# Attention blocks of one batch per core, eight key groups instead of nine, and three slots copied by register address

## What is computed

```python
xn = layernorm(x)                                    # x: 2 batches x 4096 tokens x 2048
q  = xn @ w_dq.T @ w_uq.T                            # 16 heads of 128
k, v = split(xn @ w_dkv.T @ w_ukv.T)                 # through a 512-wide latent
attn = softmax(causal(q k^T / sqrt(128))) @ v @ w_out.T
wq(w) = clip(round(w / mean|w|), -1, 1) * mean|w|    # w_gate, w_up: 8192 x 2048, w_down: 2048 x 8192
aq(x) = clip(round(x * s), -128, 127) / s, s = 127 / max|x| of the row
h  = silu(aq(xn) @ wq(w_gate).T) * (aq(xn) @ wq(w_up).T)
x  = x + attn + aq(h) @ wq(w_down).T
```

## Time and profile before

| | us |
|---|---|
| median of 3 runs | 2411.6 |
| all runs | 2411.1, 2411.6, 2578.09 |
| profiled execution, as a run | 2432.53 |
| its span on the slowest core (core 2) | 2431.0 |
| spans of the 8 cores | 2392.5 to 2431.0 |
| PE busy | 2336.6 (96%) |
| DVE busy | 1243.7 (51%) |
| ACT busy | 1166.3 (48%) |
| POOL busy | 120.9 (5%) |
| mean DMA rate | 237 GB/s |

### The profile page before, as it was taken

One profiled execution on the slowest core, in us unless ns is written; L12 is line 12 of the kernel. 1 busy time (PEld: TensorE's weight loads), 2 busy tenths in 40 slices (PEclk: granted clock), 3 DMA queues, 4 the chain that ended last, 5 costly groups with the idle time before them and its releaser, 6 DMA issues.

```text
span 2431.0 us, 41168 instructions; the slowest of 8 cores (2392.5 to 2431.0 us)
## 1 busy us (share of the span) xinstructions
PE 2336.6 (96%) x14556; PEld 1215.1 (50%) x14556; DVE 1243.7 (51%) x1668; ACT 1166.3 (48%) x1343; POOL 120.9 (5%) x227
## 2 busy tenths in 40 slices
PE   4999899999999998999999999999998999999998
PEld 2554444677777775444444444444443444444443
DVE  6883522788888874444444444444435454322222
ACT  3763311577777775445444454444542255332220
POOL 0000110000000000000000000000000100000000
PEclk9999888999999999999999999999999999999999
DMA  9875785688888837976777767777644977875551
GB/s 279 279 205 112 187 188 159 225 283 276 274 281 274 278 106 215 306 276 246 280 271 264 273 245 279 272 265 271 246 187 147 266 258 296 273 261 195 203 196 70
DMA packets 88707, 575.27 MB, mean 237 GB/s; under 512 B 10114, under 2 KB 10114, under 8 KB 25538
## 3 DMA queue, kind: packets, MB, share of 16 engines
q1 hardware_dynamic: 57490, 391.47, 46.6%
q0 software_dynamic: 31024, 181.16, 23.7%
HBM read 551.62 MB, written 48.23 MB: 247 GB/s over the span
## 4 chain that ended last, share of the span: by engine, by line
PE 80%; DMA 9%; DVE 6%; issue 3%; ACT 2%; SPq 0%; DVEq 0%; ACTq 0%; POOL 0%; POOLq 0%
PE pp L1100 36%; PE pp L1158 13%; PE pp L948 7%; PE pp L979 4%; PE pp L983 4%; PE pp L920 4%; PE pp L1043 3%; PE pp L1017 3%; DMA aos<-aob 2%; DMA hpair<-hs 2%; DMA xr<-xk 2%; DVE accTw L609 2%; PE pp L1113 1%; PE pp L1167 1%; DMA ust<-wut 1%
## 5 line engine op out<-in xcount | busy, mean ns | idle before, releaser
L1100 PE MATMUL pp<-xqfm,tw 128*128 128x512 bf16 x4096 | 886.0, 380 | 0.0
L1100 PEld LDWEIGHTS pp<-xqfm,tw 128*128 128x128 bf16 x4096 | 401.1, 98 | 484.0 <-issue 2.1
L474 ACT ACTIVATE ptile<-pp 128x512 bf16<-128x512 f32 (+3 forms) x576 | 313.3, 561 | 158.3 <-PE pp L1014 79.5
L742 DVE TENSOR_TENSOR hst<-pp,gs 128x1024 f32<-128x1024 f32 x64 | 78.4, 1224 | 351.9 <-PE pp L1100 346.6
L1043 PE MATMUL pp<-vg,ptile 128*128 128x129 bf16 x2112 | 213.8, 220 | 0.3 <-ACT ptile L474 0.2
L486 ACT ACTIVATE twi<-gst,thr 128x2048 int16<-128x2048 f32 x62 | 124.1, 2002 | 165.3 <-PE pp L1100 149.9
L494 ACT ACTIVATE gs<-gs 128x1024 f32<-128x1024 f32 x64 | 67.6, 1056 | 278.5 <-DVE gs L735 278.5
L609 DVE TENSOR_REDUCE accTw<-svr 128x1 f32<-128x1024 f32 x166 | 200.8, 1210 | 0.0
L507 ACT ACTIVATE td2i<-dst,thr 128x2048 int16<-128x2048 f32 x48 | 96.1, 2002 | 210.2 <-PE pp L1158 164.9
L1043 PEld LDWEIGHTS pp<-vg,ptile 128*128 128x128 bf16 x2112 | 151.8, 98 | 62.1 <-issue 5.5
L979 PE MATMUL pp<-ckv,wukv 128*128 128x512 bf16 x576 | 169.5, 383 | 6.4 <-DVE kg L616 5.4
(11 more groups left out here) (171 smaller groups left out, 2616.7 us busy)
## 6 DMA issues: line engine op xcount, KB each, us to landing
gst<-wgt SPq DMA_DIRECT2D x64, 1024.0 KB, 7.9
ust<-wut SPq DMA_DIRECT2D x64, 1024.0 KB, 10.7
dst<-wdt SPq DMA_DIRECT2D x64, 1024.0 KB, 5.8
sgb<-wdt POOLq DMA_DIRECT2D x62, 1024.0 KB, 11.0
svr<-wgt SPq DMA_DIRECT2D x52, 1024.0 KB, 7.5
xr<-xk SPq DMA_DIRECT2D x36, 1024.0 KB, 8.6
ssr<-wut POOLq DMA_DIRECT2D x33, 1024.0 KB, 7.8
svr<-wut SPq DMA_DIRECT2D x31, 1024.0 KB, 7.0
```

Source lines behind the costliest of these rows:

```text
L474: e.activation(out=ptile[:, n % 4, q0:512], in_=banks[3 + n % 3][:, q0:512], func=AF.Exp, scale=SCALE, bias=EXPB).then_inc(ex_s, 1)
L1100: mm = e.matmul(out=banks[b0 + half], lhsT=tw[:, n % 3, gu, fc, :], rhs=xqfm[:, 4 * half:4 * half + 4, fc, :], start=(fc == 0), stop=(fc = ...
```

## The change

Core c now takes blocks c % 4 and 7 - c % 4 of one batch, c // 4. Both need keys of the same batch, so the core projects that batch's eight groups once (NK = 4096, NKC = 32), its own two first and then the others in order. The two causal triangles and the past still make NT = 36 attention tiles a head: 8 diagonal ones ("d"), 16 of the later query block against the lower own block and the first three other groups ("f"), and 12 in three slots ("m"), in which both the key group and the query block differ by core. [...] A K or V evacuation of a later head waits for POOL's copies of the head whose buffer it overwrites. The sums of the weight blocks are divided anew: NU 8 to 12, NV 83 to 74, NS 35 to 42 (six half sums a head instead of five), NG 62 to 60, and G's sums stand two steps earlier in the gate and up loop. POOL's ssr loads are issued three a head, in one program with the copies.

```diff
-NK = 4608
-NKC = 36
+NK = 4096
+NKC = 32
+NT = 36
-TILES = [0, 4, 1, 5, 2, 6, 3, 7] + list(range(8, NKC))
+TILES = [("d", 4 * (i % 2) + i // 2) for i in range(8)] + [("f", i) for i in list(range(4)) + list(range(8, 20))] + \
+    [("m", i) for i in range(12)]
...
-    fl = [f for j in range(9) for f in (("k", h + 1, j), ("v", h + 1, j))] if h + 1 < HN else []
+    fl = [f for j in range(8) for f in (("k", h + 1, j), ("v", h + 1, j))] if h + 1 < HN else []
...
-NF, NU, NV, NS = 4, 8, 83, 35
+NF, NU, NV, NS = 4, 12, 74, 42
-V_AFTER = (1, 2, 4, 5, 7, 8, 10, 11, 13, 14, 16, 17)
-S_AFTER = (3, 9, 15, 22, 29)
+V_AFTER = (1, 2, 4, 5, 7, 8, 10, 11, 13, 14)
+S_AFTER = (3, 8, 14, 19, 25, 30)
...
         for k in range(NU):
-            e.wait_ge(qp_mm, 2 * (QCD + 2 * k))
+            e.wait_ge(qp_mm, 2 * (QCD + 3 * k // 2))
...
+        def move_slots(h):
+            e.wait_ge(kv_ev, ITEM_NO["v", h, 7])
+            if h >= 1:
+                e.wait_ge(sc_mm, NT * h)
+                e.wait_ge(pv_mm, NT * h)
+            for s in range(3):
+                e.tensor_copy(out=kdyn[:, s, :], in_=kg[:, h % 2, bass.ds(moved[s], 512)])
+                m = e.tensor_copy(out=vdyn[:, s, :, :].rearrange("p j c -> p (j c)"),
+                                  in_=vg[:, h % 2, :, :].rearrange("p j c -> p (j c)")[:, bass.ds(moved[3 + s], 520)])
+            m.then_inc(dy_p, 1)
+
         e.wait_ge(qp_mm, 2 * (QCD + FD))
-        for b in range(NS):
-            if b >= S_RING:
-                e.wait_ge(p_s, 2 * (b - S_RING + 1))
-            e.dma_start(out=ssr[:, b % S_RING, :], in_=scale_blocks[S_FIRST + b]).then_inc(s_in[b % S_RING], 16)
-        e.wait_ge(pv_mm, NKC * HN)
+        for h in range(HN):
+            if h >= 1:
+                move_slots(h)
+            for b in range(3 * h, min(3 * h + 3, NS)):
+                if b == 2:
+                    move_slots(0)
+                if b >= S_RING:
+                    e.wait_ge(p_s, 2 * (b - S_RING + 1))
+                e.dma_start(out=ssr[:, b % S_RING, :], in_=scale_blocks[S_FIRST + b]).then_inc(s_in[b % S_RING], 16)
+        e.wait_ge(pv_mm, NT * HN)
...
-            if 4 <= n < NG + 2:
-                e.wait_ge(p_g, n - 3)
-                e.dma_start(out=sgb[:, n % 2, :], in_=scale_blocks[G_FIRST + n - 2]).then_inc(pg_in[n % 2], 16)
+            if 2 <= n < NG:
+                e.wait_ge(p_g, n - 1)
+                e.dma_start(out=sgb[:, n % 2, :], in_=scale_blocks[G_FIRST + n]).then_inc(pg_in[n % 2], 16)
...
-            if 6 <= st < NG + 6:
-                n = st - 6
+            if 4 <= st < NG + 4:
+                n = st - 4
...
+            if kind != "o" and i >= 2:
+                e.wait_ge(dy_p, i - 1)
...
-            e.tensor_copy(out=qcur[:, h % 2, :], in_=qfm[:, h, :]).then_inc(qw_v, 1)
-            e.wait_ge(qw_v, h + 1)
+            e.tensor_copy(out=qcur[:, h % 2, :], in_=qfm[:, h, :]).then_inc(qc_v, 1)
+
+        def q_move(h):
+            e.wait_ge(qc_v, h + 1)
+            if h >= 1:
+                e.wait_ge(sc_mm, NT * h)
             for s in range(3):
-                c = e.tensor_copy(out=qdyn[:, h % 2, s, :], in_=qcur[:, h % 2, bass.ds(qsel[s], 512)])
-            c.then_inc(qc_v, 1)
+                m = e.tensor_copy(out=qdyn[:, s, :], in_=qcur[:, h % 2, bass.ds(qsel[s], 512)])
+            m.then_inc(dq_q, 1)
...
+            if kind == "m":
+                e.wait_ge(dy_p, h + 1)
+                e.wait_ge(dq_q, h + 1)
+                kt = kdyn[:, key // 4, 128 * (key % 4):128 * (key % 4) + 128]
...
 def halves_of(c):
-    pair = ((0, c), (1, 7 - c))
-    return pair if c >= 4 else (pair[1], pair[0])
+    return (c // 4, c % 4), (c // 4, 7 - c % 4)
```

More of the change, by code:

```diff
@@ L373, in pool_prog @@
                 e.dma_start(out=wukv[:, cc, :], in_=wukv_d[cc * 128:(cc + 1) * 128, :]).then_inc(wu_c, 16)
-        e.wait_ge(qp_mm, 2 * (QCD + FD))
-        for b in range(NS):
-            if b >= S_RING:
-                e.wait_ge(p_s, 2 * (b - S_RING + 1))
-            e.dma_start(out=ssr[:, b % S_RING, :], in_=scale_blocks[S_FIRST + b]).then_inc(s_in[b % S_RING], 16)
-        e.wait_ge(pv_mm, NKC * HN)
+        e.wait_ge(c_in, 32)
+        moved = []
+        for i in range(6, 12):
+            r = e.alloc_register("moved%d" % i)
+            e.reg_load(r, cids[0:1, i:i + 1])
+            moved.append(e.snap(r, donate=True, min_val=0, max_val=(7 * 512, 7 * 520)[i // 9]))
+        def move_slots(h):
[8 more added lines that the diff above has]
+            m.then_inc(dy_p, 1)
+        e.wait_ge(qp_mm, 2 * (QCD + FD))
+        for h in range(HN):
[8 more added lines that the diff above has]
+        e.wait_ge(pv_mm, NT * HN)
         for oc in range(6):
@@ L467, in act_prog @@
         for h in range(HN):
-            for t in range(NKC):
-                n = NKC * h + t
-                q0 = 128 * (TILES[t] % 4) if TILES[t] < 8 else 0
+            for t in range(NT):
+                n = NT * h + t
+                kind, key = TILES[t]
+                q0 = 128 * (key % 4) if kind == "d" else 0
                 e.wait_ge(sc_mm, n + 1)
@@ L708, in dve_prog @@
                 item_evac(f, 6 + ITEM_NO[f] % 2)
+                if i == (1 if h + 1 < HN else 0):
+                    q_move(h)
                 if i == 4:
@@ L993, in pe_prog, with queries @@
             fill_mm(f, 4 + i % 4, 0, 4)
[L995 to L996 removed]
+        def queries(h, kind, key):
+            if kind == "d":
                 return qcur[:, h % 2, 512 * (key // 4) + 128 * (key % 4):512 * (key // 4) + 512]
[L998 to L999 removed]
+            return qcur[:, h % 2, 512:1024] if kind == "f" else qdyn[:, key // 4, :]
         def score(n):
[L1002 to L1003 removed]
+            h, t = divmod(n, NT)
+            kind, key = TILES[t]
             if n >= 3:
                 e.wait_ge(ex_s, n - 2)
[L1006 removed]
             e.wait_ge(qc_v, h + 1)
[L1008 removed]
+            if kind == "m":
+                e.wait_ge(dy_p, h + 1)
+                e.wait_ge(dq_q, h + 1)
+                kt = kdyn[:, key // 4, 128 * (key % 4):128 * (key % 4) + 128]
+            else:
+                e.wait_ge(kv_ev, len(FIRST_ITEMS) if h == 0 else ITEM_NO["k", h, key // 4])
+                kt = kg[:, h % 2, key * 128:(key + 1) * 128]
             bank = banks[3 + n % 3]
[L1010 removed]
+            if kind == "d":
                 q0 = 128 * (key % 4)
[L1012 to L1013 removed]
+                e.matmul(out=bank[:, q0:512], lhsT=kt, rhs=queries(h, kind, key), start=True, stop=False)
                 e.matmul(out=bank[:, q0:q0 + 128], lhsT=identb[:], rhs=masksb[:], start=False, stop=True
@@ L1016, in score, with out_block @@
             else:
[L1017 to L1026, removed]
+                e.matmul(out=bank, lhsT=kt, rhs=queries(h, kind, key), start=True, stop=True).then_inc(sc_mm, 1)
+        def out_block(kind, key, b):
+            if kind == "m":
+                slot = key // 4
                 if b < 3:
-                    return pp[0].ap()[:, 129 * b:129 * b + 513 + 128][:, bass.ds(qsel[slot], 129)]
+                    return pp[0].ap()[:, 129 * b:129 * b + 641][:, bass.ds(qsel[slot], 129)]
                 return pp[1].ap()[:, 0:258][:, bass.ds(zsel[slot], 129)]
+            half = key // 4 if kind == "d" else 1
             return sums_out[1][:, half, :] if b == 3 else sums_out[2 * half][:, b, :]
         def weigh(n):
-            h, t = divmod(n, NKC)
-            key = TILES[t]
+            h, t = divmod(n, NT)
+            kind, key = TILES[t]
             e.wait_ge(ex_s, n + 1)
@@ L1037, in weigh @@
                 e.wait_ge(nr_v, 3 * (h - 1) + 2 + t)
[L1038 to L1045, removed]
+            if kind == "m":
+                vt = vdyn[:, key // 4, key % 4, 0:129]
+            else:
+                vt = vg[:, h % 2, key, 0:129]
+                if h >= 1:
+                    e.wait_ge(kv_ev, ITEM_NO["v", h, key // 4])
+                elif t == 0:
+                    e.wait_ge(vo_v, 1)
+            for b in range(key % 4 if kind == "d" else 0, 4):
+                mm = e.matmul(out=out_block(kind, key, b), lhsT=ptile[:, n % 4, 128 * b:128 * b + 128], rhs=vt,
+                              start=(t == 0 and b in (0, 3)) or (t == 1 and b == 0),
+                              stop=(t == NT - 1), skip_group_check=True)
             mm.then_inc(pv_mm, 1)
@@ L1071, in pe_prog @@
             items = items_of(h)
-            for t in range(NKC):
-                n = NKC * h + t
-                if n + 3 < NKC * HN:
+            for t in range(NT):
+                n = NT * h + t
+                if n + 3 < NT * HN:
                     score(n + 3)
@@ L1234 @@
         xo = np.concatenate([x[b0, 512 * i0:512 * i0 + 512], x[b1, 512 * i1:512 * i1 + 512]], axis=0)
-        xk = np.concatenate([xo, x[b0, :512 * i0], x[b1, :512 * i1]], axis=0)
+        rest = list(range(i0)) + list(range(i0 + 1, i1)) + list(range(i1 + 1, 8))
```

(6 more changed lines are left out.)

22 lines of the change are left out of this document (12 added, 10 removed).

## The result

The changed kernel takes 2469.6 us in the median of four executions (2468.3 to 2470.0), the kernel before 2411.4. The ratio is 1.0245, with a 95% interval of 1.0225 to 1.0265: slower, and only just beyond 2%. The forecast was 2492 us, in a range of 2435 to 2570.

A forecast was written before the change was run, and what follows sets the result against it. PE was taken to bound the kernel. From the profiled 2432.5 us, 57.9 saved, 2 added for the U ring and 136.5 for waits in heads 1 to 13 gave 2513, or 2492 for the median; range 2435 to 2570.

The forecast's parts named there:

- (a): First stage: four fewer token tiles save PE 17.4 us, and 22.6 us on core 2, whose late xr load goes.
- (b): Items of head 0 ahead of the attention: one K and one V item fewer, 2.1 us saved.
- (c): Items filled into heads 0 to 14: one K and one V item fewer, 1.75 us a head, 26.3 us saved.
- the 0.5 for DVE's copies: Heads: DVE's three query copies, moved from item 4 to item 1, would hold PE perhaps 0.5 us a head.
- (d): Start of the feed-forward part: the last head's transposes wait less for DVE, busy with weight loads; 2.5 us saved.
- (e): End of the feed-forward part: the last sgb block is summed inside the loop, so PE's wait goes; 4.4 us saved.
- The U ring: Fuller ring of sring blocks: its late twelfth block delays svr's first block after the query stage, costing 2 us.
- rival 1: Heads 1 to 13: same wait but cheap, 4.9 us a head, total 2420 us, no change that can be told; chance 0.17.
- rival 4: Heads: ACT, with 36 exps and six sums, becomes the bound of whole heads; 2379 us, within 2%; chance 0.01.

The follow-up runs named there:

- x1: Changed kernel with each head's ssr loads shifted one block, the first sum's block being asked for in the head before; 2381.6 us, ratio 0.9855 to the kernel before.
- x3: Changed kernel with ACT's six sums of a head behind tiles 13, 16, 19, 22, 28, 32, POOL untouched; 2382.6 us, ratio 0.9891 to the kernel before.
- x6: x1 with DVE's three query copies of a head behind item 4 instead of item 1; two executions take 2363.3 and 2377.3 us, no ratio given.
- x8: x1 with 8 sring blocks instead of 12 and query copies behind item 4, rerun on another chip; 2357.6 us, ratio 0.9795 to the kernel before.
- x5: x1 with the sgb blocks as in the kernel before: 62, each summed two steps later, the last after the gate and up loop; 2375.9 us.

## Why the prediction was right, point by point

**The mechanism** was right in each link: POOL's program order puts the load behind a wait for the head's start; ACT's first sum waits for it (13 times, 8.6 us in the head shown; 9 to 12 were forecast); PE stands still behind ACT's exp of tile 4; heads 14 and 15 are free of it. x1 and x3 each remove it, from the two ends.

**The sizes.** The two large terms of this chain were put too high. The six copies take 3.35 us for 4.1 (0.557 us from one to the next, between DVE's fast copy and its cast, and nearer to the cast). The first load lands in 6.0 us instead of 7.5: I reasoned that the DMA engines are quiet at a head's start and then took the median of a busy stretch all the same. They are quite idle; the columns are those of the earlier trace rows:

```profile
472.00:477.00 5.00, 4.32 (x49) 2.99 (x47) 4.92 (x13) 0.72 (x2) 4.38 (x8) 1.00 0.00 0
477.00:484.00 7.00, 0.75 (x8) 0.78 (x9) 1.80 (x3) 2.09 (x6) 0.00 (x0) 0.71 0.96 355
484.00:488.00 4.00, 4.00 (x31) 2.85 (x29) 1.56 (x3) 2.77 (x6) 0.53 (x1) 0.66 0.41 170
```

No byte moves until 477, and then 355 GB/s. The wait came to T0 + 11.2 for 13.5, and 6.6 us of standing still for 9.0. The slow matmuls behind it cost what was said: the same scores take 2.36 us in x1 (468.91 to 471.27) with waits for DVE among them and 3.60 here, 1.2 to 1.5 us; the last column but two, the granted clock, falls to 0.71 and 0.66, the means of stretches that PE spends in part at 1.2 instead of 2.4 GHz. Altogether a head was put at 30.7 + 10.5 = 41.2 us and takes 39.09. Over 13 heads that is 27 us, more than the whole miss of 22, for the other terms missed the other way: together they were put at 33 us saved and the table has 26. Two errors partly cancel, so the total is nearer than its terms, and that is luck.

On the rate of a POOL copy I had cited the Trainium skill ("GPSIMD Engine Reference", Engine selection and the cycle accounting), whose figure gives an estimate of 0.44 us for 512 elements. The rows show 0.557 us between starts, so the figure is low for this copy. Put into the sum it would have brought 2473, close to the 2469.6 measured, but only because it makes up for the load that I had put too high.

**The savings.** (a) First stage: 17.4 us on an undisturbed core and 22.6 on core 2 were forecast; core 0 gives 203.7 to 187.8 (15.9), core 2 209.6 to 186.0 (23.6). It ends at 186 to 188 on every core, so the late xr load has gone with its tile, as said. (b) and (c) hold in the main: head 14 is 1.0 us shorter, 1.75 less the 0.5 for DVE's copies and a little more, and with the copies moved (x6) 1.5 us shorter; the first items and head 0 gave 2.3 us of the 3.9 forecast. The 0.5 had the right size for a reason that was only a small part of it: the copies' place costs 0.1 us, and the rest is that the first of them is held by POOL's last (x6). (d) came true, but it is small in the table: the transposes of the last head stand behind the first gate matmul, so their wait lies in the stretch of the gate and up loop. Before, five cores had such a wait, 0.84 to 3.42 us (the earlier trace rows is core 2's); after, none has. Core 2's stretch fell from 889.8 to 884.5 us, 5.3 for the 2.5 forecast, but the median only by 1.1. What the prediction didn't have is that the last head itself became 1.8 us longer. In the changed kernel all eight cores run part of it at half clock, before only one did; on core 0 the matmuls from 978 to 985 are slow. In x8, where seven cores keep the full clock there, it still takes 25.2 us against 24.2 before; this rest is open. (e) was too small: 4.4 forecast, 7.4 measured, proved by x5. Behind that wait PE was slow too (core 2's granted clock is 0.83 in the mean from 1851.7 to 1861.7), which I had counted for the heads and forgotten here.

**The U ring.** The prediction placed its cost (2 us) at the start of head 0. There it costs nothing. It sits in the query stage, which is 5.8 us longer in the changed kernel; with 8 blocks it is 6.0 shorter than in x1. So this term was looked for in the wrong stage and was too small: I counted only the one load at the stage's end and not the three others, which run beside wring's loads in a stage in which PE already waits for these. That the loads slow each other is read from the longer wring piece; no run varies the loads alone.

**The rivals.** The cheap wait (rival 1) had the copies at 0.235 and 4.9 us a head, and would have ended the same within 2%. The truth lies between it and the forecast. In the prediction's terms it is 39.09 - 30.7 = 8.4 us a head, 7.9 of the wait (39.09 - 31.18) and 0.5 of the query copies, where the forecast had 10.5 and the text had named 8.0 as the 2% line. So the side was right with little to spare (the interval of the ratio begins at 1.0225), and some of what there is to spare comes from savings that fell short. ACT as the bound of a head (rival 4) is refuted by x1.

## What to carry to other kernels

An engine whose program only issues DMAs gives every transfer its earliest moment; the day it gets work of its own, each transfer behind that work inherits its waits, and work that is itself well hidden can still hold the loads behind it. Ask for each queue which semaphore stands in front of the next load, and when its reader wants it: one changed range bound was worth 102 us here and turned a loss of 2.4% into a gain of 1.5%. The wait of 6.7 us behind an in-order engine cost PE 7.9 us a head here, for its granted clock fell behind it (0.66 in the mean of the four us after it).

## What the runs showed of the hardware

GpSimd's copies of 128x512 bf16 with a register in the address take 0.61 to 0.62 us each and 0.557 from start to start; with 520 columns it is 0.62 or 0.63. A DVE copy of the same size within SBUF, which takes 0.28 us alone, is held until the GpSimd copy that is running ends. Started 0.07 us after it, it takes 0.70 us (12 heads of x1 on core 0); started 0.42 us after it, 0.35 us (two heads). Both times it ends 0.15 us after GpSimd's copy, so it isn't a lower rate but a wait for its end. Only one of the three query copies of a head meets a GpSimd copy, and the 0.42 us are lost once; in head 1, where two meet one, the three take 1.28 us. DVE's casts from PSUM stay at 0.68 us meanwhile (the earlier trace rows show both before). The Trainium skill ("GPSIMD Engine Reference", Key points) says that GpSimd shares its SBUF interfaces with VectorE and contends with DVE instructions in a 2-port perf mode or with two SBUF inputs. The traces agree so far as the fast copies alone are held; in which mode they run no row says. One copy held for 0.42 us behind another engine's work cost PE 0.4 us a head.
